# Slot 0 taken from eight tiles with two experts' weights split in the graph stage, and the extra slot's layer one in front of the last adjacency half

## What is computed

```python
x = x + gnn(layernorm(x), adj)          # relu(q(x) @ q(W)) -> q -> adj @ support
x = x + ffn(layernorm(x))
# ffn: logits = x @ Wr + br;  top-2 of softmax, weights normalised to sum 1
#      h = layernorm(x @ W1[e] + b1[e]) * g1[e] + be1[e];  y = gelu(h) @ W2[e] + b2[e]
#      out = sum over the two experts of weight * y
```

## Time and profile before

| | us |
|---|---|
| median of 3 runs | 511.75 (511.26 to 513.44) |
| the profiled execution | 510.59 |
| its span | 508.8 |
| PE busy | 466.0 (92%) |
| DVE busy | 353.1 (69%) |
| ACT busy | 289.3 (57%) |
| POOL busy | 236.4 (46%) |
| mean granted clock of PE | 0.975 |

### The profile page before, as it was taken

One profiled execution on the slowest core, in us unless ns is written; L12 is line 12 of the kernel. 1 busy time (PEld: TensorE's weight loads), 2 busy tenths in 40 slices (PEclk: granted clock), 3 DMA queues, 4 the chain that ended last, 5 costly groups with the idle time before them and its releaser, 6 DMA issues. The chain is left out here.

```text
span 508.8 us, 10186 instructions
## 1 busy us (share of the span) xinstructions
PE 466.0 (92%) x2297; PEld 382.8 (75%) x2298; DVE 353.1 (69%) x741; ACT 289.3 (57%) x474; POOL 236.4 (46%) x269
## 2 busy tenths in 40 slices
PE   0799999999999999677999999999999999999970
PEld 0578888878888887566888888888787887888850
DVE  5898864846689777967766686676887766786410
ACT  1666543543454533446667667668777865776440
POOL 4354420521464526546444555554545454555531
PEclk9999999999999999769999999999999999999995
DMA  8621232675796641135887776957778788464433
GB/s 298 255 84 48 77 104 84 237 228 186 260 304 247 201 154 43 46 100 192 234 250 166 215 202 136 249 107 217 236 236 255 235 276 210 93 149 73 82 49 41
DMA packets 31403, 87.25 MB, mean 171 GB/s; under 512 B 6000, under 2 KB 6144, under 8 KB 30864
## 3 DMA queue, kind: packets, MB, share of 16 engines
q1 hardware_dynamic: 17504, 56.54, 33.8%
q0 software_dynamic: 9264, 22.02, 21.2%
q10 hardware_dynamic: 4608, 8.39, 4.4%
HBM read 67.79 MB, written 19.14 MB: 171 GB/s over the span
## 5 line engine op out<-in xcount | busy, mean ns | idle before, releaser
L694 POOL DMA_INDIRECT xg<-xn_rows,tok_i x39 | 49.1, 1259 | 85.9 <-ACT gate L953 72.1
L975 ACT ACTIVATE g_sb<-ps,be_sb,g_sb 128x128 f32<-128x128 f32 x152 | 57.2, 457 | 50.9 <-PE ps L1745 50.9
L1406 DVE TENSOR_TENSOR w_lo<-w_raw,w_hi x58 | 68.3, 1219 | 8.7 <-issue 8.7
L719 POOL DMA_INDIRECT out<-y_sb,scat_i x35 | 60.8, 1738 | 23.0 <-DMA out<-y_sb,scat_i 12.9
L1413 DVE TENSOR_SCALAR h_hat<-ps,h_mv,h_rs 128x512 f32<-128x512 f32 x38 | 30.7, 808 | 47.1 <-issue 28.4
L783 ACT ACTIVATE adj_hi<-adj_raw,small 128x1024 fp32r<-128x1024 f32 x32 | 36.8, 1150 | 44.7 <-PE ps L1520 38.8
L946 ACT ACTIVATE w_hi<-w_raw x29 | 54.9, 1914 | 3.7 <-DMA w_raw<-in_w 2.4
L1083 DVE SCALAR_TENSOR_TENSOR adj_lo<-adj_raw,small,adj_hi 128x1024 fp32r<-128x1024 f32 x32 | 40.7, 1272 | 22.4 <-ACT adj_hi L783 22.3
L623 POOL TENSOR_SCALAR rstd<-mv 128x1 f32<-128x1 f32 x15 | 14.6, 976 | 76.1 <-DVE mv L1129 76.1
L1520 PE MATMUL ps<-sup,adj_hi 128*128 128x512 f32 x192 | 49.1, 398 | 0.0
L1520 PE MATMUL ps<-sup,adj_lo 128*128 128x512 f32 x192 | 49.1, 398 | 0.0
(11 more groups left out here) (215 smaller groups left out, 963.0 us busy)
## 6 DMA issues: line engine op xcount, KB each, us to landing
w_raw<-in_w SPq DMA_DIRECT2D x64, 512.0 KB
adj_raw<-in_adj_steps SPq DMA_DIRECT2D x32, 512.0 KB, 3.3
out<-x_sb ACTq DMA_DIRECT2D x16, 256.0 KB, 2.8
xn_rows<-xn ACTq DMA_DIRECT2D x16, 256.0 KB, 2.3
x_sb<-in_x SPq DMA_DIRECT2D x3, 1024.0 KB, 12.5
gw_raw<-in_gnn_w SPq DMA_DIRECT2D x1, 1024.0 KB, 5.0
x_sb<-in_x SPq DMA_DIRECT2D x2, 512.0 KB, 6.9
xg<-xn_rows,tok_i POOLq DMA_INDIRECT x39, 4.3
```

The lines of the kernel that those rows point to most:

```text
L694: return pool.indirect_dma_start(to[:, s % 2, :], None, xn_rows, bass.IndirectOffsetOnAxis(ap=tok_i[:, s:s + 1], axis=0)).then_inc(landed[ ...
L719: pool.indirect_dma_start(out, bass.IndirectOffsetOnAxis(ap=at, axis=0), y_sb[:, par, :], None, compute_op=ALU.add).then_inc(scattered[par ...
L975: ins = act.activation(g_sb[:, par, c * P:(c + 1) * P], ht_ps(par)[:, c * P:(c + 1) * P], ACT.Gelu, scale=g1_sb[:, bass.ds(e_s * C + c, 1) ...
L1406: ins = dve.tensor_tensor(w_lo[:, n, at], w_raw[:, n, :, :].rearrange("p a n -> p (a n)")[:, at], w_hi[:, n, at].bitcast(F32), ALU.subtract)
```

## The change

1. *Slot 0 is now the first page of expert 1*, also taken from the first eight tiles (padded in the same way, `early_pad`, `least` 2 for experts 0 and 1), and gathered with the extra slot's rows (`xg0`). Expert 0's ordinary page becomes slot 1. The masks of the plan (`plan_mask`, `word_of`) have one column more for this.
2. *Weights.* `e_w` and the second split of expert 0 are gone. A single region `w_split` holds both halves; expert 0's two layers and expert 1's first layer are split in windows 11 to 23 of the graph stage. Expert 1's second layer is split after it, hi by ACT after `tab_rows`, lo by DVE after slot 0's normalisation.
3. *Order.* The early gathers stand behind tile 12's scale, the tokens in window 20, the early transposes after half step 43, and early layer one, rank(3) and finish_t(14) stand between half steps 46 and 47, the last. Slot 0's layer one stands between router(15) and the last table; early layer two is moved up, its last eight products behind the compaction.
4. *Bias product.* `two_rows` and `bias_row` are given with their first two rows only (contraction of 2 in place of 128), and the memsets that zeroed the other rows are gone.
5. Batches 0 to 2 share one set of hits, and 3 and 4 have sets in the adjacency's buffers; PSUM banks of the hidden parts are exchanged.

```diff
-EARLY_ROWS_AFTER = 45
+EARLY_ROWS_AFTER = 43
-EARLY_HI_IN = {13: 0, 17: 1}
-EARLY_LO_IN = {13: (0, 0), 14: (0, 1), 15: (0, 2), 17: (0, 3), 20: (1, 0), 21: (1, 1), 23: (1, 2)}
-EARLY_PAD_IN, EARLY_TOKENS_IN = 16, 21
+EARLY_HI_IN = {11: (0, 0), 13: (0, 1), 15: (1, 0)}
+EARLY_LO_IN = {11: (0, 0, 0), 12: (0, 0, 1), 13: (0, 0, 2), 14: (0, 0, 3), 15: (0, 1, 0), 16: (0, 1, 1), 17: (0, 1, 2),
+               18: (0, 1, 3), 20: (1, 0, 0), 21: (1, 0, 1), 22: (1, 0, 2), 23: (1, 0, 3)}
+EARLY_PAD_IN, EARLY_TOKENS_IN = 16, 20
...
-    put("least", P * np.where(np.arange(E) == 0, 2, 1)[None, :])
+    put("least", P * np.where(np.arange(E) < 2, 2, 1)[None, :])
...
+            sp.wait_ge(gate_ok, 1)
             load_static(0, 2)
...
-                if t in (AHEAD + 1, AHEAD + 3):
-                    pool.memset(bias_row[(t - AHEAD - 1) // 2][:, :].bitcast(F32), 0.0).then_inc(bias_zero, 1)
...
+                pool.indirect_dma_start(xg0[:, :], None, xn_rows[0:EARLY_TILES * P, :],
+                                        bass.IndirectOffsetOnAxis(ap=e_tok[:, 1:2], axis=0)).then_inc(first_in[0], 16)
...
-                if t == T - 3:
+                if t == T - 4:
                     early_gather()
+            early_rstd()
             last_rstd(T - 1)
             row_hits(3, 0, 6)
             dense_gates(3)
             dense_gates(4)
             row_hits(4, 0, 2)
-            early_rstd()
...
             norm_xn(T - 2)
             store_xn(T - 2)
             gate_exp(3)
             finish_t(T - 2)
-            act.wait_ge(adj_mm, STEPS + WINDOWS + 1)
+            early_h_hat()
             act.wait_ge(small_in, 64)
-            split(0, 0, 48)
             act.wait_ge(xn_ok, T)
             store_xn(T - 1)
             finish_t(T - 1)
-            split(0, 1, 96)
+            slot_x_hi(0, 0)
+            slot_gate(0, 0, 1)
             gate_exp(4)
             act.preload_act_table(ACT.Gelu)
+            early_gelu()
             act.wait_ge(table_mm, 4)
             act.activation(tab_rows[:, :], table_ps, ACT.Copy).then_inc(tab_rows_ok, 1)
+            early_hi(1, 1)
             act.wait_ge(table_mm, len(BATCHES))
             act.activation(tab_sb[:, :, :], table_t_ps, ACT.Copy).then_inc(tab_ok, 1)
-            early_h_hat()
-            early_gelu()
-            split(1, 0, 48)
...
             pick(3)
             choose(3)
+            val_hits(2, 4, 6)
+            early_stats()
+            find(3)
+            gate_values(3)
+            link(dve.memset(pages_f[:, 1, E:E + 1], float(P)))
             add_tile(T - 1)
-            find(3)
+            val_hits(3, 0, 3)
             norm_last(T - 1)
             add_br(T - 2)
-            val_hits(2, 4, 6)
-            val_hits(3, 0, 6)
+            val_hits(3, 3, 6)
             add_br(T - 1)
             pick(4)
             choose(4)
-            gate_values(3)
+            slot_x_lo(0, 0)
             gate_values(4)
-            early_stats()
             find(4)
...
-            early_lo(1, 3)
-            for piece in range(C):
-                split_piece(0, 0, piece, 1)
+            early_g_lo()
...
+            slot_stats(0, 0)
             dve.wait_ge(words_mm, 1)
...
-            early_g_lo()
-            split(0, 1, 2)
...
-            slot_stats(0, 0)
-            split(1, 0, 1)
             slot_h_hat(0, 0)
+            slot_x_lo(1, 1)
+            for piece in range(C):
+                early_lo(1, 1, piece)
             slot_x_lo(2, 0)
             slot_stats(1, 1)
-            split_next(0, expert_in(word, 1), starts_in(word, 1))
...
+            def bias_product(dst, n, row):
+
+                pe.matmul(dst, two_rows[0:2, :], bias_row[n][0:2, row], start=True, stop=False)
...
-            pe.wait_ge(e_x_lo_ok, 1)
-            finish_t(T - 2)
-            rank(3)
+                if hs == 2 * WINDOWS - 2:
+                    early_layer_1()
+                    rank(3)
+                    finish_t(T - 2)
             router(T - 2)
-            early_layer_1()
             finish_t(T - 1)
-            early_layer_1_lo()
+            pe.wait_ge(logits_ok, T - 1)
+            rows_t(0, 0, 16)
+            pe.wait_ge(e_h_hat_ok, 1)
             router(T - 1)
-            early_layer_1_end()
+            first_layer_1()
             table(2)
+            early_hidden()
+            first_layer_1_lo()
+            rank(4)
             table(3)
-            rank(4)
+            first_layer_1_end()
+            early_layer_2()
...
             ins.then_inc(compact_mm, 1)
-            pe.wait_ge(e_h_hat_ok, 1)
+            early_layer_2_end()
+            pe.wait_ge(scat_ok, 1)
...
-                pe.matmul(dst, two_rows[:, :], bias_row[n][:, bass.ds((e & 3) * D, D)], start=True, stop=False)
+                bias_product(dst, n, bass.ds((e & 3) * D, D))
...
-            early_hidden()
-            early_layer_2()
-            pe.wait_ge(tok_ok, 1)
-            rows_t(0, 0, 16)
             rows_t(1, 1, 16)
-            layer_1(0, 0, 0)
             pe.wait_ge(table_ok, 1)
             word = load_plan(pe, 0)
+            layer_1(1, 1, expert_in(word, 1))
             rows_t(2, 0, 16)
-            layer_1(1, 1, expert_in(word, 1))
```

More of the change, by code:

```diff
@@ L92 @@
 FIELD = 5
-NO_WORD = sum((E - 1) << FIELD * i for i in range(5))
-BIAS_OUT_IN, WEIGHTS_IN = 6, 10
+NO_WORD = sum((E - 2) << FIELD * i for i in range(5))
+BIAS_OUT_IN, WEIGHTS_IN = 6, 8
 LN_EPS = 1e-5
@@ L304, in gnn_moe_program, with w_part, w_parts @@
         h_rs = place("h_rs", [P, 2, 4], F32)
[L305 to L312, removed]
+        assert where[0] <= end_sup
+        where[0] = x_at
+        hit_sets = [(place("hit_val0", [P, 2 * TQ, E * PAGES], F32R), hit_row0)]
+        where[0] = end_sup
+        for i in (1, 2):
+            hit_sets.append((place(f"hit_val{i}", [P, 2 * TQ, E * PAGES], F32R), place(f"hit_row{i}", [P, 2 * TQ, P], F32R)))
+        assert where[0] <= w_at
+        def w_part(n, low, e, c):
+            at = PART_AT[n][low] * (C * D) + c * D
+            return w_split[:, e % 2 * (4 * C * D) + at:e % 2 * (4 * C * D) + at + D] if isinstance(e, int) else \
+                w_split[:, bass.ds((e & 1) * (4 * C * D) + at, D)]
+        def w_parts(n, low, e, first=0, count=C):
+            at = PART_AT[n][low] * (C * D) + first * D
+            return w_split[:, e % 2 * (4 * C * D) + at:e % 2 * (4 * C * D) + at + count * D] if isinstance(e, int) else \
+                w_split[:, bass.ds((e & 1) * (4 * C * D) + at, count * D)]
         ps = ctx.enter_context(nc.psum_tensor("ps", [P, 8, D], F32))
@@ L701, in _ @@
             pool.wait_ge(tok_ok, 1)
-            for s in range(4):
+            for s in range(1, 4):
                 gather(s)
@@ new lines, in _ @@
+            add_br(T - 1)
+            pick(4)
+            choose(4)
+            slot_x_lo(0, 0)
+            gate_values(4)
+            find(4)
+            val_hits(4, 0, 4)
+            last_rows()
+            link(dve.tensor_scalar(pages_f[:, 0, 0:E], rank_ps[:, P:P + E], P // 2 - 0.5, PAGE_MAGIC, ALU.add, ALU.add))
+            link(dve.scalar_tensor_tensor(pages_f[:, 1, 0:E], pages_f[:, 0, 0:E], PAGE_MAGIC, const("least"),
+                                          ALU.subtract, ALU.max))
@@ new lines, in _, with field @@
+            link(dve.tensor_scalar(used_i[:, :], pl[:, 4:5], 4.0, None, ALU.subtract))
+            dve.tensor_scalar(pairs[:, :], used_i[:, :], 1, None, ALU.arith_shift_right)
+            slot_stats(0, 0)
+            dve.wait_ge(words_mm, 1)
+            link(dve.tensor_scalar(fields[:, :], words_ps, 1.0, None, ALU.add))
+            def field(kind, i):
+                at = kind * TAB + i
+                return fields[:, at:at + SLOTS].rearrange("p (n two) -> p n two", two=2)[:, :, 0]
+            dve.scalar_tensor_tensor(begins[:, :], field(2, 1), 2.0, field(2, 0), ALU.mult, ALU.add)
@@ L1657, in early_layer_2, with rows_t, first_part, first_layer_1 @@
                 early_part(e_y_ps, e_g_lo, 1, 0, last=True).then_inc(e_mm2, 1)
+            def rows_t(s, par, landed):
+                rows, rows_in = ((xg0, xg1)[s], first_in) if isinstance(s, int) and s < 2 else (xg[:, par, :], gathered)
+                pe.wait_ge(rows_in[par], landed)
+                for c in range(C):
+                    ins = pe.transpose(xt_ps(par)[:, c * P:(c + 1) * P], rows[:, c * P:(c + 1) * P], ident)
+                ins.then_inc(x_tp, 1)
+            def first_part(act_part, low, last=False):
+                for c in range(C):
+                    ins = pe.matmul(h_ps(0), act_part[:, 0, c * P:(c + 1) * P], w_part(0, low, 1, c),
+                                    start=False, stop=last and c == C - 1)
+                return ins
+            def first_layer_1():
+                pe.wait_ge(split_hi[0], 2)
+                pe.wait_ge(x_hi_ok, 1)
+                bias_product(h_ps(0), 0, slice(D, 2 * D))
+                first_part(xt_hi, 0)
+            def first_layer_1_lo():
+                pe.wait_ge(split_lo[0], 2)
```

(4 more changed lines are left out.)

305 lines of the change are left out of this document (136 added, 169 removed).

## The result

The changed kernel takes 535.42 us (median of 4 runs, 533.58 to 537.78) against 511.81 us for the kernel before; the ratio is 1.0458, 95% interval 1.0406 to 1.0511. It is slower by 23.6 us, where 506.0 had been forecast. The profiled execution took 537.78 us, the longest of the four; its span is 535.8.

What follows compares the result with a forecast made beforehand. Two PE-bound stretches with a gap between, so gain comes from the gap: 9.0 us at full clock less 3.2 for low clock is 5.8, 511.75 to 506.0; bias product 0. Range 500.5 to 522, the forecast's own 501 to 509.5.

Steps and rivals of the forecast that it cites:

- I take 0: First product of every layer, now 2 rows: no added PE time; upper bound 25 us if the array empties both sides.
- the rhythm: Second PE-bound stretch: PE time per slot, 6.85 us, forecast to stay so; over 7.0 would mean the bias product costs.
- Rival A: Array empties at each bias product: 531 in full, 518.5 at one side; chance 0.28, half of it at 520 or less.
- the gap's 5.8: Gap between graph stage and slots: net gain, 9.0 us at full clock less 3.2 for low clock.
- Slots and graph stage at 0: No padded slots (38 both times), and PE still without idle time in the graph stage: cost 0.
- The last half costs 3.0: Last adjacency half waits behind early layer one, rank(3) and transposes; tile 15's add at about 202.4, table's chain 3.0 us later.
- List no later than before: Token list at 217.9, as before: the 3.0 repaid by DVE order 0.8, table 0.6, remainder pieces 1.2 to 1.6.
- The clock at half, 3.2 us: PE's two waits in the gap may lower the clock: loss nothing to 6.6 us, half taken.
- rival B: The gap only moves: clock low in both waits, gain 2.4 less 1 to 2 us, 509.4 to 511.5; chance 0.15.
- the mark: Slot 2's hidden transposes, at 247.57 before; summed to 238.6 at full clock, expected at 238 to 242.
- The rhythm starts plus a fixed amount: End of kernel is when the steady slot pace of about 6.9 us starts, plus a fixed amount.
- Gather to rows, 4.6 us from the list: After the token list at 217.9, PE idles until 222.5, then takes slot 1's rows.

Runs made afterwards that it cites:

- the last kernel but one: Changed kernel with 128-row bias products and the last adjacency half in front again, then only orders on ACT, PE, POOL and DVE changed: 507.57 us, ratio 0.9909.
- the second kernel: Eight idle products in TensorE's wait for the last tile's copy, added to the 128-row kernel with last half in front and orders changed: 507.57 us, ratio 0.9918.
- the first: 24 idle products in PE's two waits of the gap, added to the changed kernel with 128-row bias products: 510.15 us, ratio 0.9956.

## Why the prediction was wrong

- **"I take 0" for the bias product on two rows** is the step that failed. It was chosen because transposes, short and long products follow each other without a pause; but these all have 128 rows, as the same paragraph said, so they bear on column counts and not on this. It is 0.33 to 0.34 us a product in the medians and 0.375 to 0.39 in the rhythm. Rival A had its cause (the change of shape), its place and nearly its size: 0.33, 25 us. The size came from the time a product is still in the array while the next streams, by its own words no price of an emptied array; that it fits is partly luck, since the rows show loads that come late at both sides. A's chance, 0.28, was too small. A term with no row that could exclude it, multiplied by 76 on an engine without idle time, decided the sign.
- **The range** took in "half of A". The row gave no reason for the half in which the array empties at one side only; the spacings show both sides, 0.17 and 0.12, and another 0.08 in the first group. The upper end had to be the full 531 and more: A's 531 also took the gap's 5.8 as gained, and only 2.5 of it came.
- **Slots and graph stage at 0**: right, 38 slots and PE 144.28 of 145 us.
- **The last half costs 3.0**: right in place, 0.6 too small. The add of tile 15 was summed at 202.4, as a wait for PE; it came at 203.00 with no idle time before it, because DVE was itself busy with the other rows in its queue until then. Putting the half back in front brought 2.5.
- **List no later than before**: wrong by 3.8 us (221.73 with the bias products on 128 rows). From the add to the last router bias it took 210.19 - 203.01 = 7.2 us and not 6.15, at low clock (with the idle products, at 1.00, it took 6.12); the rank stood on PE until 214.8 though its input was there at 213.0; and from find(4) to the list it took 1.1 us more than summed, 0.7 of them one DVE instruction beside a memset that this run has and the changed kernel has not (see the last section). The changed kernel's own list is at 221.85.
- **The clock at half, 3.2 us**: mis-sized. Both waits were as long as written (2.95 and 2.07), the clock was low after both, and most of the bound of 6.6 was paid: slot 1's layer ran 228.33 to 233.9, 5.6 us for 3.1; from its rows to its bias product another 0.7; from the add to the router bias 1.05; that is 4.3 us, and the rank's wait of 1.8 stood behind products at half pace. So the gap's gain came out as rival B's, with the sign named for it: the rhythm holds and the mark is at 245 or later. The match of 2.4 on paper with 2.5 in the medians is partly luck: the mark itself moved by only 0.9, from 247.57 to 246.67. Of the forecast's 9.0, 7.1 came at the mark (240.47) in the last kernel but one, with 128 rows, the last half in front again and the orders changed.
- **"The rhythm starts plus a fixed amount"**: not fixed. From the mark to the end of the span it is 261.2 us in the kernel before, 261.8 with 128 rows, 262.5 with the last half in front and 263.8 with the orders changed. The earlier the mark, the longer the rest, so a forecast of the mark overstates the gain; here 7.1 at the mark are 4.8 in the medians.
- **Gather to rows, 4.6 us from the list**: right, 226.26 - 221.73 = 4.5.

## What to carry to other kernels

A TensorE product on 64 rows or fewer between products on 128 costs a change of shape there and back, here 0.33 to 0.39 us around one of 512 columns. On the full 128 rows, or on 66, it cost nothing more than a plain product; making the zero rows costs POOL two memsets. When a trace shows no instance of an edit that is repeated on the bounding engine, its upper bound belongs in the forecast with a chance worthy of it, or it should be measured alone first. And when a step is brought forward on one engine, look at the in-order queue of the next: here orders on ACT and PE held back most of what the moved stages had gained.

## What the runs showed of the hardware

- 2 and 64 rows cost the same (539.53 and 538.31 us), 66 and 128 the same (512.69 and 512.75): the edge lies between 64 and 66 rows.
- The busy time of PE hides the loss: it counted 180.00 us of 180 as busy at 809 instructions, against 179.71 at 887. The loss shows in start-to-start times, in the weight loads and in the count of instructions.
- A DVE `TENSOR_SCALAR` that starts while POOL runs a memset ends about when the memset does; the DVE instructions of other kinds in these rows are not stretched. In the kernel with only the orders changed, POOL's timeline has

```profile
215.13 1.02 POOL L717 MEMSET bias_row<- 128x1024 f32 x1
```

  and a second memset from 216.10 to 217.12, and DVE's has (the first of its two took 0.16 in the kernel before):

```profile
215.36 0.88 DVE L1373 TENSOR_SCALAR pages_f<-ps 128x16 f32<-128x16 f32 x1
216.30 0.18 DVE L1374 SCALAR_TENSOR_TENSOR pages_f<-pages_f,k_sb 128x16 f32<-128x16 f32 x1
```

  In the changed kernel with 128 rows a `TENSOR_TENSOR` at 215.36 and a `TENSOR_REDUCE` at 215.62 took 0.22 us each beside a memset, and the `TENSOR_SCALAR` behind them 0.89 where it had taken 0.17. POOL's row hits beside the same value hits did not stretch them (1.44 us), two memsets did (2.67). What they share was not tried.
- Filling a wait with idle products held the clock at 1.00 in the windows of those waits, and gained nothing measurable in the medians either time. In the second kernel PE then waited for DVE (1.16 us at 211.50); in the first the mark came 1.8 us earlier and the time behind it grew by 1.5.
